# Softmax shares by broadcast loads from DRAM in place of a product, and sixteen staged chunks in four ring slots, in a fused two-layer graph network

## The reference, cut to what matters

```
h = relu(layernorm(x))
x_l = h @ W_l + b_l;  x_r = h @ W_r + b_r          # 4 heads of 32
s, d = edges and one loop per node
e = einsum(leaky_relu(x_l[s] + x_r[d], 0.2), att)  # one score per edge and head
alpha = softmax of e over the edges of one d
x = x + segment_sum(alpha * x_l[s], d) + bias
h = relu(layernorm(x)) @ W_in2f
msg = h[src] * ((ssp(attr @ Wf1 + bf1) @ Wf2 + bf2) * edge_weight)
x = x + ssp(segment_sum(msg, dst) @ Wo1 + bo1) @ Wo2 + bo2
```

## Time and profile before

| | before |
|---|---|
| median of 3 runs | 3064.7 us (3061.18 to 3067.32) |
| profiled execution: time, span | 3060.97 us, 3059.1 us |
| busy PE, DVE, ACT, POOL | 2481.3, 2262.0, 1940.3, 1870.8 us |
| mean granted clock of PE | 0.924 of 2.4 GHz |
| stage D, from the start to the first norm of stage A | 0 to about 482 us |
| stage A, 11 steps with the front half alone | about 482 to 569 us |
| stage A, 86 steps with both halves | 569 to 1397 us |
| stage A, 11 steps with the back half alone | 1397 to 1472 us |
| stages B and F | about 1472 to 2676 us, 2676 to 3059 us |

### The profile page before, as it was taken

The page is one execution under the profiler, slowest core; times in us unless marked ns, Lnnn a source line. Parts: engine busy times, 40 slices in busy tenths (PEclk is TensorE's granted clock), DMA queues, the critical chain, the costliest instruction groups (busy, mean ns, idle before and its releaser), DMA issues. The chain is left out here.

```text
span 3059.1 us, 59638 instructions
## 1 busy us (share of the span) xinstructions
PE 2481.3 (81%) x16702; PEld 1699.7 (56%) x16702; DVE 2262.0 (74%) x6291; ACT 1940.3 (63%) x4383; POOL 1870.8 (61%) x1633
## 2 busy tenths in 40 slices
PE   5988997999999998988677767777777777488877
PEld 4666663444444444445555555555555555377776
DVE  6787775788788877776777777777777777367666
ACT  4888886666566665552455555555555555289887
POOL 3455774377777777761488888888888888600000
PEclk8999999999999999987799898988999988799999
DMA  7899984254444544442456555555556556689998
GB/s 210 282 297 293 290 281 165 73 158 157 153 155 152 162 145 150 148 122 93 103 112 124 111 117 117 115 120 110 121 114 119 116 111 121 171 336 426 426 414 305
DMA packets 366956, 557.94 MB, mean 182 GB/s; under 512 B 141123, under 2 KB 218295, under 8 KB 341698
## 3 DMA queue, kind: packets, MB, share of 16 engines
q1 hardware_dynamic: 269890, 448.38, 43.9%
q0 software_dynamic: 96960, 108.35, 18.8%
HBM read 323.98 MB, written 241.26 MB: 185 GB/s over the span
## 5 line engine op out<-in xcount | busy, mean ns | idle before, releaser
L716 POOL DMA_INDIRECT sum_dram<-b_sum,b_at x392 | 639.9, 1632 | 141.9 <-issue 112.9
L634 POOL DMA_INDIRECT a_xs<-in_x,index x352 | 349.4, 993 | 114.1 <-issue 98.5
L641 POOL DMA_INDIRECT a_xd<-in_x,index x352 | 350.1, 995 | 107.3 <-issue 100.9
L704 POOL DMA_INDIRECT x_dram<-b_xo,sidx x294 | 312.6, 1063 | 106.6 <-issue 93.2
L1651 PE MATMUL bank<-b_rows,b_same 128*128 128x128 bf16 x4704 | 292.1, 224 | 0.0
L1684 PE MATMUL bank<-wo,f_ssp_out 128*128 128x128 f32 x1568 | 229.0, 292 | 69.7 <-DVE f_ssp_out L1200 68.0
L1254 ACT ACTIVATE d_n<-d_x,stat_d_shift,stat_d_rstd 128x128 f32<-128x128 f32 x686 | 283.7, 486 | 0.2 <-DVE stat_d_shift L752 0.2
L1651 PEld LDWEIGHTS bank<-b_rows,b_same 128*128 128x128 bf16 x4704 | 277.2, 101 | 0.0
L1684 PEld LDWEIGHTS bank<-wo,f_ssp_out 128*128 128x128 f32 x1568 | 204.7, 204 | 87.5 <-DVE f_ssp_out L1200 81.2
L1461 PE MATMUL bank<-ident,d_n 128*128 128x128 f32 x1184 | 191.8, 287 | 70.2 <-DMA d_n<-sum_dram 38.9
L1507 PE MATMUL bank<-wl,turned 128*128 128x128 f32 x1568 | 232.5, 292 | 11.0 <-ACT turned L1251 9.3
(11 more groups left out here) (233 smaller groups left out, 6256.3 us busy)
## 6 DMA issues: line engine op xcount, KB each, us to landing
d_x<-in_x SPq DMA_DIRECT2D x196, 256.0 KB
x_dram<-d_x SPq DMA_DIRECT2D x196, 256.0 KB
out<-d_x SPq DMA_DIRECT2D x49, 1024.0 KB, 10.4
sum_dram<-zero SPq DMA_DIRECT2D x48, 1024.0 KB
d_x<-x_dram SPq DMA_DIRECT2D x45, 1024.0 KB, 14.2
d_n<-sum_dram SPq DMA_DIRECT2D x25, 1024.0 KB, 11.9
x_end_dram<-a_xo SPq DMA_DIRECT2D x98, 256.0 KB
b_x<-x_end_dram SPq DMA_DIRECT2D x98, 256.0 KB
```

The lines of the kernel that those rows point to most:

```text
L634: pool.indirect_dma_start(a_xs[t % DEPTH][:, j * F:(j + 1) * F], None, x, column(t, j)).then_inc(gathered[t % GSEM], 16)
L641: pool.indirect_dma_start(a_xd[t % DEPTH][:, j * F:(j + 1) * F], None, x, column(t, TILES + j)).then_inc(gathered[t % GSEM], 16)
L704: pool.indirect_dma_start(x1_dram, bass.IndirectOffsetOnAxis(ap=sidx[s][:, j:j + 1], axis=0), b_xo[s][:, j * F:(j + 1) * F], None, bounds_ ...
L716: pool.indirect_dma_start(sum_dram, bass.IndirectOffsetOnAxis(ap=b_at[s][:, j:j + 1], axis=0), b_sum[s][:, j * F:(j + 1) * F], None, compu ...
```

## The change

The product with `pick` goes from PE. `shares` now writes a single `p_beta`; SP stores it to `beta_dram` once for a pack, waits until the store has landed, and for each chunk loads each of the four heads' rows with a broadcast onto 32 partitions of `a_beta` (two buffers). DVE reads `a_beta` where it read `bank7`. The signs turn: the gate comes from `gate_dram`, which holds minus `keep`, and the running sum is transposed with `neg_ident`. With `bank7` free, base product and sum alternate between `bank6` and `bank7`. On DVE the back half's three instructions move from behind `a_dif` to behind `a_u`, and `shares` from the end of its step to before `a_xo`; on PE the transposes of `a_o` move to the end of the step.

For the gathers, `STAGED` goes from 10 to 16, the staged chunks go through the last four slots (`SPARE`) in place of two, only 20 chunks (`FIRST`) are gathered in stage D besides, and the four chunks of the slots kept free are gathered when stage D's stores are done. 58 chunks are left for stage A, issued by t = 80 (`NC - LAG - 6`).

The places at which instructions move, in rows without buffer numbers. DVE before, at the end of a pack's softmax (odd step): `p_beta` is what `shares` writes, `a_dif`, `a_gate`, `a_pv`, `a_o` and `a_u` belong to the next step.

The diff, cut to its core:

```diff
-STAGED = 10
+STAGED = 16
+FIRST = 20
+SPARE = DEPTH - FIRST
...
                     if c >= 2:
                         sp.wait_ge(weighted, c - 1)
                         sp.sem_inc(sync_step, 1)
-                    sp.dma_start(a_keep[c % 2][:, :], keep_dram[c:c + 1, :].broadcast_to([P, C])).then_inc(keep_loaded[c % 2], 16)
+                    if c % PACK == 0:
+                        sp.wait_ge(rows_dve, by_dve(c // PACK, "beta"))
+                        sp.sem_inc(sync_step, 1)
+                        sp.dma_start(beta_dram[c // PACK, :, :], p_beta[:, :]).then_inc(beta_stored, 16)
+                        sp.wait_ge(beta_stored, 16 * (c // PACK + 1))
+                        sp.sem_inc(sync_step, 1)
+                    for h in range(HEADS):
+                        p = 8 * h + c % PACK
+                        sp.dma_start(a_beta[c % 2][h * HC:(h + 1) * HC, :], beta_dram[c // PACK, p:p + 1, :].broadcast_to([HC, C])).then_inc(spread[c % 2], 16)
+                    sp.dma_start(a_keep[c % 2][:, :], gate_dram[c:c + 1, :].broadcast_to([P, C])).then_inc(keep_loaded[c % 2], 16)
...
             def gather_stage(i, j):
-                slot = DEPTH - 1 - i % 2
-                if j == 0 and i >= 2:
-                    pool.wait_ge(stage_stored, 32 * (i - 1))
+                slot = DEPTH - 1 - i % SPARE
+                if j == 0 and i >= SPARE:
+                    pool.wait_ge(stage_stored, 32 * (i - SPARE + 1))
...
-            ahead += [(gather, t, h) for t in range(DEPTH) for gather in (gather_src, gather_dst) for h in range(2)]
+            ahead += [(gather, t, h) for t in range(FIRST) for gather in (gather_src, gather_dst) for h in range(2)]
             for n, (gather, t, h) in enumerate(ahead):
                 done = QUADS * (RX + 1) + n * QUADS * (NG - RX - 3) // len(ahead)
                 pool.wait_ge(d_x1_ready, done)
                 pool.sem_inc(pool_step, 1)
                 if n == TILES * STAGED:
                     store_stage(STAGED - 1)
-                    pool.wait_ge(stage_stored, 32 * STAGED)
-                    pool.sem_inc(pool_step, 1)
                 gather(t, h)
             for i in range(RN):
                 pool.wait_ge(x1_stored[i], 16 * QUADS * in_slot[i])
                 pool.sem_inc(pool_step, 1)
 
+            pool.wait_ge(stage_stored, 32 * STAGED)
+            pool.sem_inc(pool_step, 1)
+            for t in range(FIRST, DEPTH):
+                for h in range(2):
+                    gather_src(t, h)
+                    gather_dst(t, h)
             rest = [(gather, t, h) for t in range(DEPTH, NC) if t not in staged for gather in (gather_src, gather_dst) for h in range(2)]
             done = 0
             for t in range(NC):
                 early_scatters(t)
-                until = min(len(rest), -(-len(rest) * (t + 1) // (NC - LAG - 8)))
+                until = min(len(rest), -(-len(rest) * (t + 1) // (NC - LAG - 6)))
...
             def shares(b):
 
                 dve.wait_ge(rows_act, by_act(b, "rec"))
-                if b >= 2:
-                    dve.wait_ge(spread, PACK * (b - 1))
-                dve.scalar_tensor_tensor(out=p_beta[b % 2][:, :], in0=p_up[:, :], scalar=1.0, in1=p_run[:, 0:C],
+                if b >= 1:
+                    dve.wait_ge(beta_stored, 16 * b)
+                dve.scalar_tensor_tensor(out=p_beta[:, :], in0=p_up[:, :], scalar=1.0, in1=p_run[:, 0:C],
...
-                if back:
-                    s = c % 2
-                    dve.wait_ge(spread, c + 1)
-                    dve.wait_ge(keep_loaded[s], 16 * (c // 2 + 1))
-                    dve.scalar_tensor_tensor(out=a_gate[:, :], in0=bank[7][:, :], scalar=1.0, in1=a_keep[s][:, :],
-                                             op0=ALU.add, op1=ALU.mult)
-                    dve.tensor_tensor(a_pv[:, :], bank[7][:, :], a_xs[c % DEPTH][:, :], ALU.mult).then_inc(weighted, 1)
-                    dve.wait_ge(weighted, c + 1)
-                    if c >= 1:
-                        dve.wait_ge(sum_scan, c)
-                    if c >= 2:
-                        dve.wait_ge(out_turned, c - 1)
-                    dve.tensor_tensor_scan(a_o[s][:, :], a_gate[:, :], a_pv[:, :], a_o[1 - s][:, C - 1:C] if c else 0.0,
...
+                if back:
+                    s = c % 2
+                    dve.wait_ge(spread[s], 64 * (c // 2 + 1))
+                    dve.wait_ge(keep_loaded[s], 16 * (c // 2 + 1))
+                    dve.scalar_tensor_tensor(out=a_gate[:, :], in0=a_beta[s][:, :], scalar=-1.0, in1=a_keep[s][:, :],
+                                             op0=ALU.add, op1=ALU.mult)
+                    dve.tensor_tensor(a_pv[:, :], a_beta[s][:, :], a_xs[c % DEPTH][:, :], ALU.mult).then_inc(weighted, 1)
+                    dve.wait_ge(weighted, c + 1)
+                    if c >= 1:
+                        dve.wait_ge(sum_scan, c)
+                    if c >= 2:
+                        dve.wait_ge(out_turned, c - 1)
+                    dve.tensor_tensor_scan(a_o[s][:, :], a_gate[:, :], a_pv[:, :], a_o[1 - s][:, C - 1:C] if c else 0.0,
+                                           ALU.mult, ALU.add).then_inc(sum_scan, 1)
                 if packed and phase == 1:
                     carry_max(b)
                 if packed and phase == 2:
                     run_max(b)
                 if t + LEAD < NC:
                     sums_a(t + LEAD)
+                if packed and phase == 3:
+                    shares(b)
                 if back:
                     dve.wait_ge(out_turned, c + 1)
                     if c >= 4:
                         dve.wait_ge(end_stored[s], 16 * ((c - 4) // 2 + 1))
                         dve.wait_ge(early_scattered[s], 16 * EARLY[s] * ((c - 4) // 2 + 1))
-                    dve.tensor_tensor(a_xo[c % 4][:, :], bank[6][:, :], a_xd[c % DEPTH][:, :], ALU.add).then_inc(x1_ready, 1)
+                    dve.tensor_tensor(a_xo[c % 4][:, :], bank[6 + c % 2][:, :], a_xd[c % DEPTH][:, :], ALU.add).then_inc(x1_ready, 1)
...
-                    b = c // PACK
-                    n = c % PACK
-                    pe.wait_ge(rows_dve, by_dve(b, "beta"))
-                    if c >= 1:
-                        pe.wait_ge(weighted, c)
-                    pe.matmul(bank[7][:, :], pick[:, n * P:(n + 1) * P], p_beta[b % 2][:, :], start=True, stop=True).then_inc(spread, 1)
                     hd = a_hd[c % (LAG + 1)]
-                    if c >= 1:
-                        pe.wait_ge(x1_ready, c)
-                    pe.matmul(bank[6][:, :], ones3[:, 0:P], bias_d3[:, :, :].rearrange("k j f -> k (j f)"), start=True, stop=False)
+                    to = bank[6 + c % 2]
+                    if c >= 2:
+                        pe.wait_ge(x1_ready, c - 1)
+                    pe.matmul(to[:, :], ones3[:, 0:P], bias_d3[:, :, :].rearrange("k j f -> k (j f)"), start=True, stop=False)
                     for j in range(TILES):
-                        last = pe.matmul(bank[6][:, j * F:(j + 1) * F], hd[:, j * P:(j + 1) * P], wl[:, :], start=False, stop=False)
+                        last = pe.matmul(to[:, j * F:(j + 1) * F], hd[:, j * P:(j + 1) * P], wl[:, :], start=False, stop=False)
...
-                if back:
-                    pe.wait_ge(sum_scan, c + 1)
-                    for j in range(TILES):
-                        last = pe.matmul(bank[6][:, j * F:(j + 1) * F], a_o[c % 2][:, j * P:(j + 1) * P], ident[:, :],
-                                         start=False, stop=(j == TILES - 1))
-                    last.then_inc(out_turned, 1)
...
                     turn_dst(t + 1)
+                if back:
+                    pe.wait_ge(sum_scan, c + 1)
+                    for j in range(TILES):
+                        last = pe.matmul(bank[6 + c % 2][:, j * F:(j + 1) * F], a_o[c % 2][:, j * P:(j + 1) * P], neg_ident[:, :],
+                                         start=False, stop=(j == TILES - 1))
+                    last.then_inc(out_turned, 1)
```

More of the change, by code:

```diff
@@ L119, in gnn @@
         neg_att = sb("neg_att", [P, PR + 8])
-        pick = sb("pick", [PR, PACK * P])
+        neg_ident = sb("neg_ident", [P, P])
         own_col = sb("own_col", [PR, 8])
@@ L182, in gnn @@
         a_keep = two("a_keep", [P, C], BF16)
+        a_beta = two("a_beta", [P, C])
         a_gate = sb("a_gate", [P, C])
@@ L194, in gnn @@
         p_up = sb("p_up", [PR, C])
-        p_beta = two("p_beta", [PR, C])
+        p_beta = sb("p_beta", [PR, C])
         p_col = sb("p_col", [PR, 8])
@@ L225, in gnn @@
             bo2_all = at("bo2_all", [P, F])
+            pick = at("pick", [PR, PACK * HEADS])
             p_own0 = at("p_own0", [PR, 16])
+            gate_b = at("gate_b", [P, C], BF16)
         with ExitStack() as place:
@@ L298, in gnn @@
         rows_dve = sem("rows_dve"); rows_act = sem("rows_act"); row_mm = sem("row_mm")
-        spread = sem("spread"); based = sem("based")
+        beta_stored = sem("beta_stored"); spread = sems("spread"); based = sem("based")
```

(13 more changed lines are left out.)

13 lines of the change are left out of this document (8 added, 5 removed).

## The result

The changed kernel takes 3138.65 us (median of four, 3133.64 to 3142.04) against 3062.94 (four runs of the kernel before): ratio 1.0251, interval 1.0221 to 1.0281, slower by 2.5%. The forecast was 3110 us, within 3052 to 3160. The profiled span went from 3059.1 to 3135.7 us, 76.6 more.

A forecast was written before the change was run, and what follows sets the result against it. Prediction: PE and POOL bound stage A before, DVE's chain afterwards. Stage A +45, stage D +6 and tail -5 give +46 us on the profiled 3060.97, so 3107, or 3110 us for the median; range 3052 to 3160.

The forecast's parts named there:

- Stage A: The 86 steps with both halves: 142.1 us for fourteen steps, 873 us for 86 against 828.3, +45.
- Plain steps: DVE in stage A, start to start: 8.18 us for even steps and 9.90 for odd ones, 18.08 a pair.
- The round trip: At a pack's start, shares stored and loaded in 7.3 us; DVE stands still 3.3 or 1.6 us at alternate packs.
- the clock: PE's clock falls behind stalls of DVE in stage A: 2.0 us per fourteen steps, between none and 5.1.
- the pack operations: Softmax of two packs within fourteen steps of stage A: left at 8.6 us, as in the kernel before.
- the bound of 11.8: Upper bound in us for the softmax of two packs: eight of fourteen steps would each lose 0.4 at a_u.
- The order on PE: PE's transposes for a_xo in stage A run beside 1.55 us of statistics on DVE.
- POOL: Gathers and scatters in stage A: 9.92 us a turn at the least before, 8.9 after, no longer the bound.
- Stage D and the tail: Stage D +6 us from more staged chunks (0 to 14.5); tail -5 from the dropped product (-11 to +7).
- Rival 1: Round trip at pack starts lands beside the step, so stall and its clock go: 3048 us, faster; chance 0.17.
- Rival 3: Loads at pack starts come late, gate rows up to 7.0 us at every pack: 3157 to 3176 us; chance 0.12.
- SBUF operands: Gate and a_pv read shares from SBUF, not PSUM: nothing charged; the skill's estimate was 0.065 us less, twice a step.

The follow-up runs named there:

- run 85: Not a run label: "in that run 85 steps" counts 85 steps in the changed kernel with LAG 12 in place of 11, 3098.6 us.
- the good orders: Changed kernel with the old instruction orders on DVE and PE put back and LAG 12 in place of 11: 3028.3 us, 0.9889 of the kernel before.

## Why the prediction was right, and where it was short

- **In sum.** The mechanism came as forecast, and its size was too low: +46 us forecast, +76.6 measured between the profiled spans. Stage A has +74.3 for +45, stage D +4.9 for +6, the tail +0.8 for -5, and stages B and F, with the steps of the front half alone, are 3.4 shorter.
- **Plain steps.** 8.18 and 9.90 us were forecast, 18.08 a pair; 8.28 and 9.79 were measured, 18.07. The empty wait at `a_u` and the kept wait of ACT for `stat_e_var` are both in the trace.
- **The round trip.** Forecast 7.3 us and stalls of 3.3 and 1.6; measured 7.5 in the median, 7.7 at 867 us, and stalls of 3.46 and 1.67 in the packs from 728 to 875 us. Its parts were off both ways, so that the sum comes so near is in part luck: the store landed in 1.6 us in the median, not the 2.6 of the earlier trace rows, which is a row of POOL's queue, and the last load took 4.1 at 867 us, not 3.2. The gate's waits were 34.6 us in all, 14 of them. The formula of the Trainium skill, "DMA: Bandwidth & Descriptors", section "Anatomy of one DMA — SWDGE (gpsimd) path", is for DMAs that GpSimd issues. These are SP's, so its 2.15 us are not put to a test here; the store's 1.6 and the 3.4 of a gate row in the median lie on either side.
- **What was undersized: the clock and the pack operations.** From the gate at 728.50 to that at 874.91, fourteen steps take 146.4 us. Less 126.6 for plain steps and 5.1 of stalls that leaves 14.7, where the step "the pack operations I leave at 8.6" and the clock's 2.0 made 10.6. 4.8 us on the whole fourteen (146.9 in the mean over the stage, 142.1 forecast) is 29 us in 86 steps, all of the difference in stage A. About 4.1 of the 14.7 stand behind stops of PE, where I took 2.0 for the clock: behind the stop of 4.6 us up to 731.16 `a_xo` comes 0.7 later after its gate than in plain steps, behind that of 2.0 us up to 802.56 `a_u` comes 1.6 later after `a_dif`, and behind that of 5.2 us up to 857.40 it comes 1.8 later. The first two in DVE's timeline, and the windows behind these two stops (the third is in the windows above); the clock is 0.50 in all three:

```profile
733.27 0.69 DVE L1091 TENSOR_TENSOR a_xo<-bank,a_xd 128x512 f32<-128x512 f32 x1 [0.63 <-PE bank L1612]
809.08 0.75 DVE L1062 SCALAR_TENSOR_TENSOR a_u<-bank,cols,a_xs 128x512 f32<-128x512 f32 x1 [3.77 <-ACT a_xs L1344]
```

```profile
731.20:735.00 3.80, 3.80 (x15) 3.14 (x16) 2.77 (x14) 0.26 (x2) 0.09 (x1) 0.50 1.04 404
803.60:806.80 3.20, 3.20 (x12) 2.31 (x11) 1.71 (x6) 1.65 (x4) 1.92 (x2) 0.50 0.95 305
```

The other 10.6 are the softmax, in place of 8.6 and below the bound of 11.8. ACT's four passes ahead of `a_hd` are no part of what was added: the wait of 3.08 us that they leave before `a_dif` at every second pack is in the kernel before as well, and so in the 8.6. What was added shows best where DVE has `p_run` and `p_q`, 1.9 us, in a step without the sums. This step takes 10.68 us from `a_dif` to `a_dif` in the changed kernel (773.75 to 784.43), 2.6 more than a plain one of its kind. In the kernel before it took 9.22 (874.92 to 884.14), 0.6 more, because the wait before `a_dif`, 1.62 us in a plain step, fell to 0.50, and the wait before `a_u` went. I did not count this slack. `a_dif` in the kernel before, in that step, in the step with passes and sums, and in a plain step:

```profile
884.14 0.69 DVE L1026 TENSOR_TENSOR a_dif<-a_hd,bank 128x512 f32<-128x512 f32 x1 [0.50 <-ACT a_hd L1301]
951.04 0.69 DVE L1026 TENSOR_TENSOR a_dif<-a_hd,bank 128x512 f32<-128x512 f32 x1 [3.08 <-ACT a_hd L1301]
977.84 0.69 DVE L1026 TENSOR_TENSOR a_dif<-a_hd,bank 128x512 f32<-128x512 f32 x1 [1.62 <-ACT a_hd L1301]
```

The shares of the clock and of the softmax are read from one stretch of one trace; no run takes them apart.

- **The order on PE.** The prediction took the transposes of `a_o` to run beside the statistics, and in the changed kernel `a_xo` waits for them for 1.4 us in all from 600 to 1300 us. That their new place costs 36 us once DVE's order is undone (3064.2 against 3028.3 with `LAG` 12) it did not see.
- **POOL.** That POOL bounded the kernel before and no longer bounds the changed one was right: the staging alone takes 26 us off the kernel before, and its removal from the changed kernel lengthens stage A by 4 only.
- **Stage D and the tail.** +6 and -5 forecast, +4.9 and +0.8 measured. That the first agrees is in part luck: stage D ends up to 8 us apart in traces of kernels that share it. The saving in the tail did not come; why stays open.
- **Rival 1** had the round trip as the deciding mechanism, and 3048 us when hidden. With it hidden the time was 3098.6; to come below 3048 the two orders have to go as well (3028.3). Without stalls I had 9.66 a step; in that run 85 steps took 850.2 us, 10.0 each, short by the same undersized terms. **Rival 3** did not come: the landing had a median of 3.4 us, no longer than 5.6, and no round trip took more than 8.8.
- **SBUF operands.** The gate takes 0.681 us in the median against 0.684 from PSUM; the 0.065 less by the Trainium skill, "VectorE: DVE Perf Modes", section "The TRN2 errata — SBUF-src ops pay a fixed extra latency per instruction", did not appear.

## What to carry to other kernels

Taking work off the busiest engine pays only if no chain is as long right behind it: write the next engine's step out, start to start, with every wait that stays. An instruction that fills a wait is free; behind the wait it can cost its whole length, and here three such instructions, with the transposes moved on PE, cost 70 us (3098.6 against 3028.3, both with `LAG` 12). A wait that seems idle may be what hides something else: the softmax grew when the waits of the kernel before went. A value that goes through DRAM took 6.6 to 8.8 us here and needs as much lead; one more step of lag gave it. And a change of two parts has to be taken apart: the staging alone, without the loads, gives 0.8% of the 1.1% that the good orders gain.

## What was not expected of the hardware

Two stops of PE of nearly one length can leave different clocks. In the run with `LAG` 12 (windows, columns as in the earlier trace rows) PE waited 2.13 us up to 897.61 and 2.01 us up to 909.30:

```profile
897.60:901.00 3.40, 3.39 (x7) 1.68 (x8) 1.19 (x5) 2.50 (x7) 2.49 (x4) 0.61 0.76 272
...
909.30:912.70 3.40, 3.40 (x11) 1.53 (x12) 3.22 (x5) 3.37 (x8) 2.73 (x2) 1.00 0.96 381
```

The clock behind the first is 0.61, behind the second 1.00. Steps of this place in later packs take 11.6 to 12.4 us there, and 10.7 for the most part in the changed kernel. What decides stays open.
